# A two-layer graph network on one core: GpSimd waits twice a pair of blocks, and the first layer counts its groups of target nodes in another order

## What is computed

```python
# layer 0, on h = relu(layernorm(x)); row = src, col = dst (sorted)
ef  = relu(edge_attr @ We1 + be1) @ We2 + be2
ef  = ef * sigmoid(ts @ Wt + bt)
msg = relu(concat([h[row], ef], 1) @ Wn1 + bn1) @ Wn2 + bn2
x   = x + segment_sum(msg, col) + h
# layer 1, on h = relu(layernorm(x))
agg = segment_sum(h[src], dst)
x   = x + relu(relu((h + agg) @ W1 + b1) @ W2 + b2)
```

## Time and profile before

| | |
|---|---|
| median of 3 runs | 3862.44 us (3859.89 to 3878.18) |
| the profiled execution, its own time | 3848.36 us |
| its span, first to last instruction | 3846.6 us |
| busy in the span | PE 71%, DVE 51%, ACT 26%, POOL 54% |
| mean granted TensorE clock | 0.797 of full speed |

### The profile page before, as it was taken

The page is one execution under the profiler, slowest core; times in us unless marked ns, Lnnn a source line. Parts: engine busy times, 40 slices in busy tenths (PEclk is TensorE's granted clock), DMA queues, the critical chain, the costliest instruction groups (busy, mean ns, idle before and its releaser), DMA issues.

```text
span 3846.6 us, 58359 instructions
## 1 busy us (share of the span) xinstructions
PE 2746.8 (71%) x14587; PEld 1705.2 (44%) x14588; DVE 1970.9 (51%) x4080; ACT 1013.4 (26%) x1000; POOL 2069.2 (54%) x2109
## 2 busy tenths in 40 slices
PE   4877677767677777778777877776663766667667
PEld 3444444444344444435444444443342544455445
DVE  8654555555555555555555555564674333333333
ACT  3332333323233333323233332322231101111112
POOL 7655555555455555555555554545336455555553
PEclk8788888887888788878887887877886767777778
DMA  5433333333333333333334343333213333333331
GB/s 169 123 119 111 113 120 110 111 120 105 117 101 120 110 109 116 120 107 115 112 114 116 104 124 109 114 109 104 79 51 128 99 96 122 123 120 98 111 121 63
DMA packets 234934, 426.49 MB, mean 111 GB/s; under 512 B 86462, under 2 KB 147470, under 8 KB 234542
## 3 DMA queue, kind: packets, MB, share of 16 engines
q0 software_dynamic: 74160, 151.46, 15.3%
q1 hardware_dynamic: 109552, 178.49, 14.1%
q10 hardware_dynamic: 50928, 93.34, 6.8%
HBM read 363.64 MB, written 59.42 MB: 110 GB/s over the span
## 4 chain that ended last, share of the span: by engine, by line
issue 27%; PE 21%; SPq 20%; DVE 13%; another core or an unknown queue 10%; DVEq 7%; DMA 1%; ACT 0%; POOL 0%; ACTq 0%
SPq L486 14%; PE ps L1000 9%; PE ps L900 4%; SPq L482 3%; DVE nodes L1270 3%; PE ps L858 3%; DVEq L1194 2%; PE ps L868 2%; DVEq L1250 1%; DVE arena L1270 1%; DVEq L1267 1%; PE ps L990 1%; DVE big L1220 1%; DVE hot L1225 1%
## 5 line engine op out<-in xcount | busy, mean ns | idle before, releaser
L592 POOL DMA_INDIRECT big<-table,idx x2064 | 2001.8, 970 | 1670.8 <-issue 593.7
L900 PE MATMUL ps<-nodes 128*128 128x500 bf16 x1280 | 433.6, 460 | 324.5 <-DVE nodes L1270 191.4
L858 PE MATMUL ps<-arena,we 128*128 128x512 f32 x784 | 496.0, 762 | 28.5 <-issue 16.2
L713 ACT ACTIVATE big<-big 128x1024 f32<-128x1024 f32 x196 | 207.1, 1057 | 1151.1 <-DVE big L1220 828.3
L1270 DVE TENSOR_SCALAR nodes<-iota_k,win_off,nodes 128x500 bf16<-128x500 f16 x1280 | 461.6, 413 | 0.5 <-issue 0.5
L879 PE MATMUL ps<-hot,big 128*128 128x64 f32 x3136 | 414.2, 288 | 52.8 <-issue 28.2
L879 PEld LDWEIGHTS ps<-hot,big 128*128 128x128 f32 x3136 | 406.0, 208 | 57.6 <-issue 55.7
L1220 DVE TENSOR_TENSOR big<-ps,big 128x1024 f32<-128x1024 f32 x180 | 219.5, 1219 | 354.0 <-issue 287.4
L849 PE MATMUL ps<-arena,we 64*128 64x512 f32 x784 | 258.0, 727 | 199.9 <-DMA arena<-in_ea 187.0
L1267 DVE TENSOR_TENSOR nodes<-iota_b,nodes 128x384 bf16<-128x384 f16 (+1 forms) x492 | 245.5, 499 | 223.0 <-remote 182.6
L1202 DVE TENSOR_TENSOR acc<-ps,acc 128x128 f32 x392 | 114.1, 291 | 458.4 <-remote 398.6
(11 more groups left out here) (152 smaller groups left out, 2604.4 us busy)
## 6 DMA issues: line engine op xcount, KB each, us to landing
arena<-in_ew SPq DMA_DIRECT2D x196, 512.0 KB
arena<-in_ea SPq DMA_DIRECT2D x196, 256.0 KB
counts_d<-arena ACTq DMA_DIRECT2D x192, 245.0 KB
acc<-counts_d ACTq DMA_DIRECT2D x15, 2940.0 KB
big<-table,idx POOLq DMA_INDIRECT x2064
nodes<-table SPq DMA_DIRECT2D x2048, 0.5 KB
table<-big SPq DMA_DIRECT2D x7, 672.0 KB, 3.0
idx<-in_src SPq DMA_DIRECT2D x260, 4.0 KB
```

The costliest lines, as they stand in the source:

```text
L592: pool.indirect_dma_start(to(u, q, t)[0:n], None, table, bass.IndirectOffsetOnAxis(ap=idx[0:n, u, at:at + 1], axis=0))\
L858: i = pe.matmul(p_ef[q], we2[:, :], hid[:, q, :], start=True, stop=True)
L900: m = pe.matmul(to, hots[:, t, :], keys[:, t, :], start=False, stop=True, skip_group_check=True)
```

## The change

Two things, both in the first layer. `early_group` reads the group of u = 0 from a table, `FIRST_GROUPS`: bodies 1 to 6 take the groups 47 to 42 as before; bodies 7 to 40 take alternately one of the groups 33 down to 17 and one of the large groups of `MIDDLE`; bodies 41 to 48 take the groups 41 to 34. So the visits of u = 0 are 1 in the bodies 1 to 7; 3 in the bodies 10, 18 and 32; 4 in 12 and 36; 5 in 28 (group 1); 11 in 22 (group 0); 1 in 9, 15, 41, 42, 43, 45, 46 and 47; and 2 in all others. And the gathers of a pair are issued in two halves of four, the second behind a wait for `agg_mm` of pair N-3, which TensorE gives in step N ahead of the group's counting. The last two bodies have neither wait.

```diff
+MIDDLE = (12, 6, 2, 9, 14, 4, 11, 0, 13, 7, 1, 10, 5, 15, 3, 8, 16)
+FIRST_GROUPS = tuple(range(LC - 1, 41, -1)) + sum(((33 - i, g) for i, g in enumerate(MIDDLE)), ()) + tuple(range(41, 33, -1))
...
         def early_group(b, u):
-            return b + (u * LC - 1) if u else LC - b
+            return b + (u * LC - 1) if u else FIRST_GROUPS[b - 1]
...
+            def gather_half(b, u, q, last):
+                if last and u == RING - 1:
+                    gather_block(table0, to_rows, u, q, gathered, EDGE_TILES - (NTILE - (2 - q) * TB))
+                elif isinstance(b, int) and (b * RING + u, q) in FETCHED:
+                    gather_block(table0, to_rows, u, q, gathered, TB, (TB - 1) * q)
+                else:
+                    gather_block(table0, to_rows, u, q, gathered)
...
                     if not free:
                         pool.wait_ge(ef_mm, b * (2 * RING) + 2 * u)
                     pool.sem_inc(pairs_begun, 1)
-                    if last and u == RING - 1:
-                        gather_last(table0, to_rows, gathered)
-                    elif isinstance(b, int) and b * RING + u in dict(FETCHED):
-                        gather_rest(table0, to_rows, u, dict(FETCHED)[b * RING + u], gathered)
-                    else:
-                        gather_pair(table0, to_rows, u, gathered)
+                    gather_half(b, u, 0, last)
+                    if not free:
+                        pool.wait_ge(agg_mm, b * RING + (u - 2))
+                    pool.sem_inc(pairs_begun, 1)
+                    gather_half(b, u, 1, last)
```

More of the change, by code:

```diff
@@ L98 @@
 assert all(fetched_until(u, q, NBODY) == FETCHED_EACH for u in range(RING) for q in (0, 1))
+MIDDLE = (12, 6, 2, 9, 14, 4, 11, 0, 13, 7, 1, 10, 5, 15, 3, 8, 16)
+FIRST_GROUPS = tuple(range(LC - 1, 41, -1)) + sum(((33 - i, g) for i, g in enumerate(MIDDLE)), ()) + tuple(range(41, 33, -1))
+assert sorted(FIRST_GROUPS) == list(range(LC))
 NP3 = 3
@@ L599, in gather_pair @@
                     gather_block(table, to, u, q, landed)
-            def gather_rest(table, to, u, half, landed):
-                for q in (0, 1):
-                    gather_block(table, to, u, q, landed, TB, (TB - 1) * q if q == half else None)
             def gather_last(table, to, landed):
```

## The result

Of six runs each, the changed kernel takes **3690.09 us** (3673.03 to 3727.89), the kernel before 3861.16 us beside it (3849.41 to 3878.18). The ratio is **0.957**, 95% interval 0.951 to 0.963: 4.3% faster. The forecast was 3794 us, 1.8%, with a range down to 3720. So the sign was right, and more than half of the gain was not foreseen.

The account below looks back on a forecast made before the run. SyncE's issuing of single-row DMAs was taken as the bound. The terms -56 (end), 0 (visits), 0 and -12 (second wait) gave -68 us: 3780 profiled, 3794 us as a median, 1.8% faster, range 3720 to 3905.

Parts of the forecast that it names:

- SyncE is never held by anybody: it takes the pairs at its own pace, and the others can only be as fast as that: First layer, 97 to 2550 us: SyncE's issuing of single-row DMAs sets the pace, 13.9 us a pair, 55.8 a body.
- that loop: GpSimd's gathers and TensorE's held messages: four 12.55 us cycles plus 8.0 for the opening step, 58.2 us a two-visit body.
- the second wait: Middle of each gated pair: lets agg_mm out 5 us earlier behind the opening step; counted 0 there, -12 us through SyncE.
- Up to 91 us: Bodies 10 to 44: most that the second wait could give back on TensorE's and VectorE's side, set against the visits' 52.
- The visits in the middle: 24 visits moved into bodies 7 to 41: 52 us of TensorE and VectorE work, expected hidden, 0, bounds 0 and +52.
- the rival on the visits: Bodies 7 to 41: second wait shortens no step, the 52 us stand in the open; 3858 us, no change; chance 0.16.
- The end, -56: Bodies 45 to 48: 19 visits at u = 0 leave them, 279 to 221 us; -56 us, bounds -54 and -58.
- SyncE gets much faster: Gated pairs: nearly every one is cut, leaving SyncE a whole microsecond more quick time; -168 us, 3694 us; chance 0.11.
- GpSimd as the bound: Gated pairs: two blocked stops each, 15.2 us against 13.9; 4030 us, or 3918 at half the pairs; chance 0.18.
- The slower moved gathers: Second half of each pair: VectorE's window operations slow the moved gathers by 0.08 us each; +55, 3849 us; chance 0.03.
- Fair sharing: SyncE's rows: only the amount GpSimd moves slows them, so cuts change nothing; 3806 us; 0.12, within the forecast's own chance.

Follow-up runs that it names:

- wait_alone: The changed kernel with the old order of the groups, so only the second wait is new against the kernel before: 3720.69 us, 0.963.
- The halved rows: SyncE fetches rows for 8 tiles, not 16, all up to pair 92: 1.004 in the kernel before, 0.948 in the changed one, 0.952 with wait and old order.
- half of the cuts: Kernel before plus the second wait in pairs u = 0 and u = 1 alone: 1.000, 1.000, 0.999 without the hold; 0.973 with it.
- wait_earlier: Kernel before plus the second wait in every gated pair, its count lowered by one so it is there long before: 1.001.

## Why the prediction was right and wrong, step by step

**"SyncE is never held by anybody: it takes the pairs at its own pace, and the others can only be as fast as that": wrong, and all of the miss hangs on it.** That it waits for nobody was true. But without any rows to issue it did not make the others faster (1.004, and 56.2 us a body), and its pace went from 13.9 to 13.1 us a pair in wait_alone ((2400.0 - 98.8) / 176), again almost unheld. That it was a close second is my reading, not shown. The bound was the loop of GpSimd's gathers and TensorE's held messages, which the prediction had worked out, and then laid aside behind SyncE. Its own sum had the warning in it: it put that loop at 58.2 us for a body of two visits, more than SyncE's 55.8, so the loop, and not SyncE, was the slower of the two. The terms that failed by this are the second wait, put at 0 and -12 where it took 157.2 us off, and the visits, put at 0.

**The second wait: mechanism right, size wrong, by the cap.** Said: five us earlier at the step behind the opening, a body of two visits from 58.2 to 53.2 us. Measured: that step went from 14.8 to 9.7 us, and the body from 56.0 to 52.1. "Up to 91 us" was only credited against the visits; uncapped it was 131.7 us in the 35 bodies 10 to 44, and 157.2 up to body 44 in all. Bodies 4 to 9, where the prediction expected nothing of it, shortened too, 56.2 to 52.4 us in wait_alone; but the same bodies took 53.4 to 54.7 in kernels that had no stop there at all, so between 1 and 4 us of a body are the wait's, and no run settles how much.

**The visits in the middle, "0, bounds 0 and +52": wrong, near or above the upper bound.** 36.0 us without the wait, 57.3 with it. (The terms that the prediction names make 4.5 + 8.8 + 8.6 + 25.7 = 47.6 us, not 52.) The argument that SyncE's pace hides them fell with the first step. So the rival on the visits was right on them, and wrong in that the wait "shortens no step".

**The end, -56: right.** -58.8 in the changed kernel, 220.2 us against "221", by the sum of 16 steps, one held step and one visit. The parts were off and cancelled: bodies 45 and 46 took 47.4 and 45.1 us where four cycles are 50.2, body 47 took 72.5 for 67.7 (its held step 33.5 for 30) and body 48 took 55.2 for 53.1. So that it came to within 1 us was partly luck.

**"SyncE gets much faster", 3694 us: right in the number and not in the cause.** It gave its 112 us to SyncE's quick time between gathers. The halved rows show that such time bought nothing before the change; only with the wait may it be worth some 1%. SyncE's last row, forecast at 2540 us, was out at 2462.8.

**The other rivals.** GpSimd as the bound: not seen. In three pairs of four the only stop is the one in the middle, and `ef_mm` was out in time; at u = 1 both stops stay. The slower moved gathers: the mean gather went from 970 to 979 ns, 19 us in all 2,064, well below the 0.08 us that the rival put on each moved one, and no loss of time from it was seen. Fair sharing: in the condition without the hold SyncE's twelve rows take 6.23 us beside unbroken gathers, so the amount that GpSimd moves is not what makes them slow. The rule named beside it in the prediction (the Trainium skill, "DMA: Bandwidth & Descriptors", section "Issuing engines are not separate DMA queues") is not contradicted in that condition, and does not explain the 18.77 us of the other.

**The sum in the profiled executions:** end -59, visits +57, wait -157, together -159 in the first layer (2674.62 against 2833.26); 7 us are lost again behind it, where nothing was changed. There the executions differ by as much as 21 (wait_alone), and in the condition without the hold the new order costs the second layer 10 us. Whether the order brings anything beside the wait stays open: 0.957 against 0.963 have overlapping intervals, and the traces say 2 us.

## What to carry to other kernels

An engine that never waits need not be the bound: before you cap every gain at its pace, take some of its work away, or at least ask how early its results are used. Where a long unbroken run of descriptor-writing gathers stands beside an engine that announces results, put a stop at the point where such a result is just due. Here no stop was added: the one at the start of a pair moved to its middle, GpSimd's idle time before its gathers fell from 1670.8 to 1502.2 us (wait_alone), and a body got 3.9 us shorter. It paid only where the messages are held (0.963 there, 1.000 for half of the cuts in the other condition), so look at the waits on TensorE's semaphores against the end of the gathers' runs first.

## What the runs showed of the hardware that was not expected

- The hold is a condition that comes and goes, not a property of the program. The same kernel before took 3864 us, 2838 us and, later, 3796 us (medians), each within 1.4% on its occasion; beside kernels on a chip numbered 7 it took 2836 and 3796 us an hour apart, on one numbered 6 3864 and 2838 us. Gathers take the same time in both. What makes it, no run here shows.
- In it, three things come together. TensorE's messages mostly wait for the gathers to pause: 405 of 462 that fall into a run are late in the kernel before, none of 1,088 in the other condition, and none of ScalarE's and VectorE's in either. Twelve of SyncE's rows take 12.0 us in the median and up to 21, in place of 6.3. And the second layer, whose instructions this change does not touch, takes 1,013 us in place of 788, from the last weighing to the end of the span.
- In the condition with the hold, GpSimd's instruction without a stop between gathers does not let the messages out (wait_earlier, 1.001). Stops of 2 to 3 us do.
